# Layer 2 attention's middle blocks written out, and a new order around the last block of layer 0

## The reference, cut to what matters

```python
# layer 0: one head over 256 channels; RMS norm, modulation by scale and shift
h = film(rmsnorm(x, norm1_w), cond, film1_w, film1_b)
Q, K, V = h @ q_w + q_b, h @ k_w + k_b, h @ v_w + v_b
x = x + softmax(Q @ K.T / 16) @ V @ proj_w + proj_b
h = film(rmsnorm(x, norm2_w), cond, film2_w, film2_b)
x = x + gelu(h @ mlp_w1 + mlp_b1) @ mlp_w2 + mlp_b2
# layer 2: 16 heads of 64 channels, so W_qkv is 256 x 3072
q, k, v = split(modulate(layernorm(x), sh_msa, sc_msa) @ W_qkv)
x = x + g_msa * (softmax(q @ k.T / 8) @ v @ W_out + b_out)
```

## Time and profile before

| what | value |
| --- | --- |
| median of 3 runs | 2108.38 us |
| the profiled execution's own time | 2108.39 us |
| its span, first to last instruction | 2106.6 us |
| mean granted TensorE clock | 0.988 |
| TensorE matmul busy | 1998.5 us (95%) |
| TensorE weight load busy | 1639.1 us (78%) |
| VectorE busy | 1301.5 us (62%) |
| ScalarE busy | 1018.7 us (48%) |
| GpSimd busy | 439.5 us (21%) |

### The profile page before, as it was taken

The page is one execution under the profiler, slowest core; times in us unless marked ns, Lnnn a source line. Parts: engine busy times, 40 slices in busy tenths (PEclk is TensorE's granted clock), DMA queues, the critical chain, the costliest instruction groups (busy, mean ns, idle before and its releaser), DMA issues.

```text
span 2106.6 us, 44526 instructions
## 1 busy us (share of the span) xinstructions
PE 1998.5 (95%) x15460; PEld 1639.1 (78%) x15460; DVE 1301.5 (62%) x2506; ACT 1018.7 (48%) x1623; POOL 439.5 (21%) x409
## 2 busy tenths in 40 slices
PE   8989998989899999999999989998999999999998
PEld 7977887777777888877777777776888778787887
DVE  6665665777775656545544555555666777775664
ACT  4436555565643333335444444445446645554453
POOL 4441113445430101011111111111011321210000
PEclk9989999999999999999999999999999999999999
DMA  6000000111110000000000000000000000000000
GB/s 230 16 15 8 7 11 28 46 37 45 37 38 11 20 10 20 10 11 7 2 5 7 6 7 1 5 4 13 6 7 8 11 6 10 10 0 11 20 20 30
DMA packets 23959, 42.06 MB, mean 20 GB/s; under 512 B 2354, under 2 KB 13106, under 8 KB 23474
## 3 DMA queue, kind: packets, MB, share of 16 engines
q1 hardware_dynamic: 23858, 40.65, 5.8%
HBM read 28.06 MB, written 4.19 MB: 15 GB/s over the span
## 4 chain that ended last, share of the span: by engine, by line
PE 80%; DVE 8%; issue 7%; ACT 3%; POOL 1%; DVEq 0%; DMA 0%; ACTq 0%; POOLq 0%; SPq 0%
PE psum L633 21%; PE psum L635 19%; PE psum L634 19%; PE psum L728 4%; PE psum L741 3%; PE psum L675 3%; PE psum L760 2%; PE psum L826 2%; DVE xn L1149 2%; PE psum L774 2%; PE psum L717 1%; DVE pb L1220 1%; DVE mx L1217 1%; PE psum L564 1%; DVE h_lo L1170 1%
## 5 line engine op out<-in xcount | busy, mean ns | idle before, releaser
L633 PE MATMUL psum<-h_hi,w_lo 128*128 128x512 f32 x1056 | 433.9, 411 | 18.3 <-DVE h_lo L1170 7.6
L635 PE MATMUL psum<-h_hi,w_hi 128*128 128x512 f32 x1056 | 414.6, 393 | 0.0
L634 PE MATMUL psum<-h_lo,w_hi 128*128 128x512 f32 x1056 | 413.5, 392 | 0.0
L1272 DVE TENSOR_TENSOR hid_lo<-hid,hid_hi 128x512 fp32r<-128x512 f32 x256 | 193.0, 754 | 264.2 <-ACT hid_hi L1029 264.1
L1029 ACT ACTIVATE hid_hi<-hid 128x512 fp32r<-128x512 f32 x256 | 161.8, 632 | 219.4 <-PE psum L635 128.1
L1352 POOL TENSOR_TENSOR rstd<-ms,half_t 128x4 f32<-128x4 f32 x64 | 65.9, 1030 | 920.1 <-DVE ms L1144 474.6
L633 PEld LDWEIGHTS psum<-h_hi,w_lo 128*128 128x128 f32 x1056 | 199.2, 189 | 67.5 <-issue 16.5
L1217 DVE TENSOR_REDUCE mx<-psum 128x8 f32<-128x512 f32 x192 | 132.1, 688 | 168.0 <-PE psum L717 114.9
L635 PEld LDWEIGHTS psum<-h_hi,w_hi 128*128 128x128 f32 x1056 | 198.9, 188 | 44.0
L634 PEld LDWEIGHTS psum<-h_lo,w_hi 128*128 128x128 f32 x1056 | 199.8, 189 | 34.7
L1024 ACT ACTIVATE hid<-psum,vec 128x512 f32<-128x512 f32 x192 | 131.7, 686 | 163.9 <-PE psum L635 152.8
(11 more groups left out here) (143 smaller groups left out, 3675.0 us busy)
## 6 DMA issues: line engine op xcount, KB each, us to landing
swapped<-rows SPq DMA_DIRECT2D x64, 128.0 KB, 2.0
stage<-in_w_dram SPq DMA_DIRECT2D x24, 256.0 KB, 2.7
stage<-in_w_dram SPq DMA_DIRECT2D x8, 512.0 KB, 3.6
out_dram<-xres SPq DMA_DIRECT2D x8, 512.0 KB, 2.9
xres<-in_x_dram SPq DMA_DIRECT2D x1, 3072.0 KB, 15.3
modw_mod<-in_modw_dram SPq DMA_DIRECT2D x2, 1536.0 KB, 17.4
stage<-in_w_dram SPq DMA_DIRECT2D x8, 384.0 KB, 3.2
stage<-in_w_dram SPq DMA_DIRECT2D x8, 192.0 KB, 2.4
```

Of the source, the lines that this page charges most:

```text
L633: nc.tensor.matmul(dst, s_lo, m_hi, start=start and j == 0, stop=False)
L634: nc.tensor.matmul(dst, s_hi, m_lo, start=False, stop=False)
L635: ins = nc.tensor.matmul(dst, s_hi, m_hi, start=False, stop=stop and j == len(pairs) - 1)
L1272: nc.vector.tensor_tensor(hid_lo[:, slot, :], hid32[:, slot, :], hid_hi[:, slot, :].bitcast(F32), ALU.subtract).then_inc(sem["hid"], 1)
```

## The change

Two edits. Phase 4 joins phase 0 in having its middle blocks written out on all engines, with constants in place of registers. At the end of phase 0, GpSimd's `share` of block 7 waits for h of the MLP's first block, and the `bias` behind it in GpSimd's queue with it; and `up 0` and `up 1` are both issued behind `divide` (7), ahead of `probs_t` (7), on all engines. The remaining lines of the diff let one stage be followed by two and drop a test that is not needed where the block is always a number.

```diff
+UNROLLED = (0, 4)
+
-UP_AFTER = {0: [("probs_t", 0), ("pv", 0)], 1: [("merge", 0), ("proj", 0)],
+UP_AFTER = {0: [("divide", 0), ("divide", 0)], 1: [("merge", 0), ("proj", 0)],
             2: [("pv", 7), ("proj", 7)], 3: [("merge", 0), ("proj", 0)]}
...
-                            if PHASES[ph][0] == "mlp" and (e_s, e_k) in UP_AFTER[PHASES[ph - 1][1]]:
-                                stage_of(ph, "up", UP_AFTER[PHASES[ph - 1][1]].index((e_s, e_k)), 0)
+                            if PHASES[ph][0] == "mlp":
+                                for n, place_of in enumerate(UP_AFTER[PHASES[ph - 1][1]]):
+                                    if (e_s, e_k) == place_of:
+                                        stage_of(ph, "up", n, 0)
...
-                if engine is None or ph == 0:
+                if engine is None or ph in UNROLLED:
                     for i in range(1, blocks - 1):
...
-                    if not isinstance(b, int) or b < blocks - 1:
+                    if b < blocks - 1:
                         pool.wait_ge(sem["h"], n_at("h", ph, b + 1, 2))
...
                 elif s == "share":
                     if is_first(b):
                         pool.wait_ge(sem["x_done"], n_at("x_done", ph, 0, 1))
+                    if ph == 0 and b == blocks - 1 and phases > 1:
+                        pool.wait_ge(sem["h"], n_at("h", 1, 0, 2))
                     split_next(ph, b)
```

## The result

The changed kernel takes 2081.60 us (median of four runs, 2081.16 to 2083.48) against 2106.66 for the kernel before (four runs, 2096.86 to 2109.8), a ratio of 0.9897 with a 95% interval of 0.9871 to 0.9923. The profiled execution took 2081.59 us, its span is 2079.2. Beside the last experiment both kernels ran again on another chip: 2081.62 (2080.36 to 2083.0) against 2108.5 (2106.6 to 2113.25), ratio 0.9875, 0.9859 to 0.9892.

A forecast was written before the change was run, and what follows sets the result against it. TensorE, busy 95% of the span, was taken as the bound. 18.8 us from phase 4 written out plus 10 at the end of layer 0 gave 28.8 off 2108.39, so 2079.6 us; range 2072 to 2095.

The forecast's parts named there:

- part A: Phase 4's loop written out: six passes take 371.8 us instead of 390.57, 18.8 us less.
- part B: End of layer 0, with the added wait and moved up products: about 10 us less.
- The stops go: Phase 4: two TensorE stops behind the loop's returns, low clock included, vanish in straight code; 12.27 us.
- The registers: Phase 4: written-out passes drop register instructions and waits on registers, 1.1 us a pass, 6.5 in all.
- The norm free of GpSimd: End of phase 0: VectorE's MLP norm takes 1.92 us instead of 5.43, so the turn starts 3.5 us earlier.
- v ends at 139.65: Behind the turn, block 7's v ends at 139.65 instead of 145.93, with 2.8 us less from half clock gone.
- pv at 146.0: End of layer 0: ScalarE's gelus and casts ahead of the copy to `pt` hold pv, idle 1.05 us.
- No half clock at the end of layer 0: Turn and pv run at full clock, half clock's 5.65 us taken away; down 0 at 150.5 instead of 161.06.
- rival (c): End of layer 0 gains about 6 us, as the clock falls again and GpSimd's queue is the wait; 2083.6, 16%.
- (a): Phase 4's stops come from the amount of code, not the jump, and return twice; 2091.9 us, 7%.
- (b): Register instructions hide nothing; something else holds TensorE in phase 4's blocks 1 to 6; 2086.1 us, 7%.
- (d): Slower: straight-line fetch falls behind TensorE in all six middle blocks, 6.1 us each; 2116.4 us, 4%.

The follow-up runs named there:

- the last experiment: Changed kernel with phase 6 also written out, block 7's bias behind divide and up 1 behind probs_t at layer 0's end; 2076.61 us.
- experiment 5: Changed kernel with phase 4's middle blocks back in a loop whose jump is announced; 2090.01 us.
- (6): Changed kernel with phase 4 in a loop of three passes, two blocks in each; 2100.94 us.
- (7): Changed kernel with phase 2 looping in two passes of three blocks instead of six of one; 2082.73 us, a single time.
- experiment 9: Changed kernel with the bias of layer 0's last block behind divide in GpSimd's queue; 2085.98 us, a single time.
- experiment 1: Kernel before with only phase 4's middle blocks written out, end of layer 0 as before; 2088.2 us, ratio 0.9909.
- experiment 3: Kernel before with only GpSimd's share waiting for h; phase 4 in its loop, up 0 and up 1 in their old places; 2098.26 us, single time.

## Why the prediction was right

2079.6 us was forecast, 2081.6 measured; 28.8 us of gain forecast for the profiled execution, 26.8 measured. Of the 2.0 missing, 0.1 are part A's, 1.4 part B's, and the rest lies outside the span, which is shorter by 27.4. Step by step:

- **The stops go (12.3 us).** Right: 12.6 by experiment 5, which takes them away and nothing else. The reading, code fetched again behind a jump, holds: with the jump announced no packet comes in over five passes (experiment 5), with a body twice as long both returns stop (6), and a body three times as long makes a stop in phase 2 (7). Two of its readings were loose. The row for the second pass ends at 1110 us, and two packets come in before that pass is over; and these two are among the nine that it put behind the return, so seven are behind it.
- **The registers (6.5 us).** Right: 6.1 between experiment 5 and the written-out form, and paid without a return too (6). A written-out pass was worked out at 61.96 from two stretches and takes 61.97.
- **The norm free of GpSimd; turn at 132.75.** Right: 1.92 us and 133.00. The turn's start is 0.25 us later than forecast, and each later start here counts from there.
- **v ends at 139.65, h at 138.8, share at 140.85, divide at 144.3, probs_t at 144.35.** Measured: TensorE idle from about 140.0, h at 138.6, share at 140.6, divide at 144.0, probs_t at 144.04. The share's and the bias's time behind the added wait were the ones read from before.
- **pv at 146.0, held by ScalarE.** Right: 146.24, and experiment 9 shows that it is ScalarE and not GpSimd.
- **No half clock at the end of layer 0.** Wrong in this execution, and it is the term that was mis-sized: pv took 3.54 us, down 0 came at 152.49 instead of 150.5, 8.6 us of gain instead of 10. The prediction had it as rival (c) at 16%, with 6 us for the gain; what it cost was one stretch of 3.4 us. In the six other profiles with the same end no half clock follows the stop, and the 17.8 us from the turn to down 0 are the 17.75 forecast. So the forecast of 10 was the better one, and the profiled execution was the one of seven that missed it. What a single profile shows here is in part luck, on both sides: the kernel before had two stretches of 6.8 us in its profile, experiment 1 has two of 3.4 with the same instructions, and 5.65 us of what part B's cross-check adds up come from the longer ones. Against experiment 1's down 0 the changed kernel's gain would be 5.9 us instead of 8.6.
- **The rivals.** (a) falls with experiments 1 and 5, (b) with experiment 1's passes, (d) with the six straight passes, none of which shows a stop.

Open is why some returns of a loop of this size stop and others don't: two of five in three profiles, one in experiment 3, always with two packets of code just ahead. No experiment set the place of the loop's code, which would be the way to tell.

## What to carry to other kernels

In this kernel a loop with a long body pays twice: for registers in each pass (1.0 us in 63), and, where its code comes in again behind a return, for a stop with half clock behind it. Both can be read before anything is built, from "issue" waits behind a return with instruction packets around them, and from a block that is already written out. But measure phase by phase: in the MLPs writing out gained nothing that shows, and in phase 2 it changed which of GpSimd and VectorE was held and lost time. And read more than one profile before a few microseconds of half clock are put down to an edit.

## What was not expected of the hardware

- A stop of 1.5 us draws a stretch of half clock in one execution and none in another, with the same instructions ahead of it (3.54 and 2.00 us for the same eight matmuls). Of the seven stops of 1.8 to 2.4 us ahead of phase 2's blocks 1 to 7, two are followed by half clock in the changed kernel's profile and three in that of before.
- A jump announced at the top of the loop did not only hide the fetch: in five passes no packet came, where the loop before had 19.
- Written out, phase 2 lost 0.7 us a pass where GpSimd's cast went through and VectorE was held, though both start within 0.05 us of each other in either kernel. It is the same interference as the one that the added wait removes at the end of layer 0.
